# Layernorm of a linear-attention and FFN kernel: feature-major statistics on TensorE, or token-major bn_stats with a DMA transpose

## What is computed

```python
xn = _layernorm(x, axis=-1)                      # mean and variance over 1024 features
# recurrence, per batch: q, k, v = xn@Wq, xn@Wk, xn@Wv (64 wide); g = sigmoid(xn@Wg + bg)
#   S = decay * S + outer(k*g, v*g); out_t = q_t @ S;  s = outs @ Wo + bo
# feed-forward, int8-valued weights stored as int32, scale 1/127, hidden 3072:
#   h = silu(xn@wg.T) * (xn@wu.T);  g = silu(h@wd.T)
return x + s * g
```

## Time and profile before

| | us |
|---|---|
| median of 2 runs (716.69 and 722.12) | 719.41 |
| the profiled execution's own time | 720.41 |
| its span on the slowest core (core 2) | 718.8 |
| spans of the 8 cores | 708.5 to 718.8 |
| TensorE matmul busy | 602.2 |
| VectorE busy | 265.7 |
| ScalarE busy | 169.4 |
| GpSimd busy (issuing DMAs for the most part) | 73.4 |

### The profile page before, as it was taken

How to read it: one execution, slowest core, us unless ns; L and a number is a source line. 1 busy time by engine, 2 the same in 40 slices (tenths; PEclk the granted TensorE clock), 3 DMA queues, 4 the chain that set the end, 5 groups by cost and what they waited for, 6 DMA issues and landing times.

```text
span 718.8 us, 8478 instructions; the slowest of 8 cores (708.5 to 718.8 us)
## 1 busy us (share of the span) xinstructions
PE 602.2 (84%) x2939; PEld 288.4 (40%) x2996; DVE 265.7 (37%) x477; ACT 169.4 (24%) x268; POOL 73.4 (10%) x146
## 2 busy tenths in 40 slices
PE   0451877969884997988889999899999999999997
PEld 0320433535452444543434343344444444444443
DVE  2457076748886225453221222221112211122222
ACT  0541165545662021300100000111111111101100
POOL 5010212101110100110100000011111111000000
PEclk9975979889997899999999999999999999999999
DMA  8970788675651421323323132354544545012232
GB/s 165 177 119 1 111 117 133 101 125 67 109 89 31 77 40 31 50 45 54 45 44 118 59 118 72 104 81 67 87 68 79 83 66 88 1 58 101 76 117 89
DMA packets 24747, 58.63 MB, mean 82 GB/s; under 512 B 2753, under 2 KB 2881, under 8 KB 24706
## 3 DMA queue, kind: packets, MB, share of 16 engines
q0 software_dynamic: 19584, 39.85, 36.4%
q1 hardware_dynamic: 4608, 16.78, 6.6%
q10 hardware_dynamic: 514, 1.45, 0.8%
HBM read 89.53 MB, written 8.39 MB: 136 GB/s over the span
## 4 chain that ended last, share of the span: by engine, by line
PE 69%; DMA 11%; DVE 9%; issue 6%; ACT 3%; POOL 1%; DVEq 0%; ACTq 0%; POOLq 0%
PE pb L712 39%; PE pb L780 23%; DMA xstage<-xfm 7%; DMA xstage<-xpfm 4%; DVE abig L394 3%; PE pb L506 2%; DVE xn L398 1%; DVE wd_bf L398 1%; PE pb L796 1%; ACT xsqf L307 1%; PE pb L539 1%; ACT abig L814 1%; PE pb L423 1%; POOL wd_bf L279 1%; POOL gubf L679 1%
## 5 line engine op out<-in xcount | busy, mean ns | idle before, releaser
L712 PE MATMUL pb<-xn,gubf 128*128 128x512 bf16 x1495 | 351.0, 392 | 37.2 <-DVE xn L398 23.1
L712 PEld LDWEIGHTS pb<-xn,gubf 128*128 128x128 bf16 x1536 | 152.4, 101 | 223.0 <-issue 61.0
L780 PE MATMUL pb<-wd_bf,h_bf 128*128 128x512 bf16 x752 | 169.0, 379 | 9.5 <-ACT abig L814 5.9
L739 DVE SCALAR_TENSOR_TENSOR h_bf<-pb,sgbf 128x512 bf16<-128x512 f32 x96 | 66.1, 691 | 247.6 <-PE pb L712 213.7
L734 ACT ACTIVATE sgbf<-pb 128x512 bf16<-128x512 f32 x96 | 56.9, 593 | 275.6 <-PE pb L712 275.6
L780 PEld LDWEIGHTS pb<-wd_bf,h_bf 128*128 128x128 bf16 x768 | 74.4, 98 | 101.4 <-issue 12.8
L679 POOL DMA_DIRECT2D gubf<-wgu x96 | 50.9, 537 | 484.3 <-PE pb L712 369.2
L823 DVE TENSOR_TENSOR abig<-abig,pb 128x512 f32<-128x512 f32 x32 | 22.0, 688 | 137.9 <-ACT abig L814 82.0
L814 ACT ACTIVATE abig<-pb 128x512 f32<-128x512 f32 x32 | 19.1, 598 | 167.0 <-PE pb L780 167.0
L307 ACT ACTIVATE xsqf<-xstage 128x1024 bf16<-128x1024 bf16 x32 | 31.9, 1048 | 67.0 <-DMA xstage<-xpfm 34.2
L158 ACT ACT_TABLE_LOAD x32 | 41.1, 1283 | 0.6
(11 more groups left out here) (85 smaller groups left out, 206.3 us busy)
## 6 DMA issues: line engine op xcount, KB each, us to landing
gubf<-wgu POOLq DMA_DIRECT2D x96, 256.0 KB, 4.9
xtmt<-xtm SPq DMA_DIRECT2D x16, 512.0 KB, 4.0
out<-xtmt SPq DMA_DIRECT2D x16, 512.0 KB, 2.9
wd_bf<-wdt POOLq DMA_DIRECT2D x24, 256.0 KB, 8.8
xstage<-xfm POOLq DMA_DIRECT2D x8, 512.0 KB, 11.8
xstage<-xpfm POOLq DMA_DIRECT2D x8, 512.0 KB, 9.2
abig<-wqk ACTq DMA_DIRECT2D x1, 512.0 KB
xtmt<-wkvg ACTq DMA_DIRECT2D x1, 512.0 KB
```

The costliest lines, as they stand in the source:

```text
L712: e.matmul(out=o, lhsT=gu_bf[gpar][:, gu * 1024 + dc * 128: gu * 1024 + (dc + 1) * 128], rhs=xn[:, dc * N + half * 1024 + nh * 512: dc * N ...
L739: e.scalar_tensor_tensor(out=h_bf[:, hc * 1024 + nh * 512: hc * 1024 + nh * 512 + 512], in0=a, scalar=QS, in1=sg_bf[:, sgp * 512:(sgp + 1) ...
L780: e.matmul(out=o[:, dh * 512:(dh + 1) * 512], lhsT=h_bf[:, hc * 1024 + nc2 * 128: hc * 1024 + (nc2 + 1) * 128], rhs=wd_bf[:, hc * 1024 + d ...
```

## The change

The layernorm is turned to the token-major layout, in 32 tiles of 128 tokens.

- The host sends x once, token-major, as `xttm`: 32 tiles of 128 tokens by 1024 features, f32, own tokens first. The residual at the end reads the same tensor.
- `lnA_p(q)` loads a tile on SyncE's queue, with no cast, three tiles in flight.
- `lnB_p(q)`: two bn_stats of 128x512 on VectorE. `lnC_p(q)`: bn_aggr, a Sqrt of 128x1 on ScalarE, a reciprocal of 128x1, and one tensor_scalar of 128x1024 (f32 to bf16) that subtracts the mean and multiplies. There are two buffers `xhb` for its result, so tile q waits for the transpose of tile q-2.
- `lnD_p(q)`: SyncE issues a DMA transpose (SBUF to SBUF, 128x1024 bf16) into `xn`, or for a previous tile into `wd_bf`, waits for its completion, and raises the semaphore `YT` with a nop. What waited for VectorE's last operation on a tile waits for `YT` now (`f_e1`, `kvg_chunk`, `sum_chunks`, `qk_pass`).
- Gone are the squares, the 256 statistics matmuls, the variance on 128x256, the long reciprocal and the four TENSOR_TENSOR operations for each 256 tokens.
- The order of the tiles is 8 own, 16 previous, 8 own (`TOR`). The decay chain and the casts of the small weights become entries of `pre` (`decay_pre` at k = 3, `stage_pre` at k = 4), behind the first tiles.
- `pre` has two entries for a tile of 128 tokens. Slice 0 of the feed-forward stands behind the transpose of tile 3, slice 1 behind that of tile 7, and slices 2 to 24 carry the rest of layernorm.

The core of the diff (`decay_pre` holds the old decay chain, with a vector of ones of its own in place of `vtmp`; `kvg_chunk` holds the old matmuls and copies of `lnB_c`):

```diff
-    xfm = nc.dram_tensor("xfm", [8, 128, NDC * TL], F32, kind="ExternalInput").ap()
-    xpfm = nc.dram_tensor("xpfm", [8, 128, NDC * TL], F32, kind="ExternalInput").ap()
-    xtm = nc.dram_tensor("xtm", [N, D], F32, kind="ExternalInput").ap()
+    xttm = nc.dram_tensor("xttm", [32, 128, D], F32, kind="ExternalInput").ap()
...
-        xstage = [E_(nc.sbuf_tensor(f"xstage{i}", [128, NDC * TL], BF16)) for i in range(3)]
-        xsq_f = [E_(nc.sbuf_tensor(f"xsqf{i}", [128, NDC * TL], BF16)) for i in range(2)]
-        m_sb = [E_(nc.sbuf_tensor(f"msb{i}", [128, TL], F32)) for i in range(2)]
+        xts = [E_(nc.sbuf_tensor(f"xts{i}", [128, D], F32)) for i in range(3)]
+        xhb = [E_(nc.sbuf_tensor(f"xhb{i}", [128, D], BF16)) for i in range(2)]
+        stc = [E_(nc.sbuf_tensor(f"stc{i}", [128, 16], F32)) for i in range(2)]
+        ones_r = E_(nc.sbuf_tensor("ones_r", [1, 128], F32))
...
+        for dst, src in [(dec_s[:], dec), (bgs_s[:], bgs)]:
+            s.op(lambda e, d_=dst, s_=src: e.dma_start(out=d_, in_=s_), dDC, 16)
+        dec_done = dDC.n
...
+        def decay_pre():
+            s.wait(dDC, dec_done)
...
+            t.wait(S, s_ld)
+            t.wait(V, v_const)
+            t.op(lambda e: e.matmul(out=pb[3][:, 0:1], lhsT=ones_r[:],
+                                    rhs=ld_s[:], start=True, stop=True))
...
+        def stage_pre():
+            v.wait(dSM, smalls_done)
+            v.op(lambda e: e.memset(outsa[M:M + 1, :], 1.0))
+            v.op(lambda e: e.memset(S_bf[0][:], 0.0))
+            v.op(lambda e: e.tensor_copy(out=wqk_bf[:], in_=abig[:]))
+            v.op(lambda e: e.tensor_copy(out=wkvg_bf[:, 0:1024],
+                                         in_=xtmt[0][:]))
+            v_w1 = v.op(lambda e: e.tensor_copy(out=wkvg_bf[:, 1024:1280],
+                                                in_=xtmt[1][:, 0:256]), V, 1)
+            s.wait(V, v_w1)
+            s.op(lambda e: e.dma_start(out=abig[0:M + 1, :], in_=wob),
+                 dSM, 16)
+            smalls2 = dSM.n
+            v.wait(dSM, smalls2)
+            v.op(lambda e: e.tensor_copy(out=wob_bf[:], in_=abig[0:M + 1, :]),
+                 V, 1)
+            stg8["v_wsmall"] = V.n
...
+        TOR = list(range(8)) + list(range(16, 32)) + list(range(8, 16))
+
+        def lnA_p(q):
+            p3 = q % 3
+            if q >= 3:
+                y.wait(V, ap32[q - 3])
+            y.op(lambda e, d_=xts[p3][:], s_=xttm[TOR[q]]:
                  e.dma_start(out=d_, in_=s_), dX[p3], 16)
+            x_issue[q] = dX[p3].n
+
+        def lnB_p(q):
+            p3 = q % 3
+            par = q % 2
+            v.wait(dX[p3], x_issue[q])
+            if q >= 2:
+                v.wait(S, s_sig[q - 2])
+            v.op(lambda e, o=stc[par][:, 0:6], a=xts[p3][:, 0:512]:
+                 e.bn_stats(out=o, in_=a))
+            v_red[q] = v.op(lambda e, o=stc[par][:, 6:12],
+                            a=xts[p3][:, 512:1024]:
+                            e.bn_stats(out=o, in_=a), V, 1)
+
+        def lnC_p(q):
+            p3 = q % 3
+            par = q % 2
+            c = stc[par]
+            v.wait(V, v_red[q])
+            v_agg = v.op(lambda e, o=c[:, 12:14], a=c[:, 0:12]:
+                         e.bn_aggr(out=o, in_=a), V, 1)
+            s_pre("Sqrt")
+            s.wait(V, v_agg)
+            s_sig[q] = s.op(lambda e, o=c[:, 14:15], a=c[:, 13:14]:
+                            e.activation(out=o, in_=a, func=AF.Sqrt,
+                                         bias=eps_c[:]), S, 1)
+            v.wait(S, s_sig[q])
+            v_rc = v.op(lambda e, o=c[:, 14:15]:
+                        e.reciprocal(out=o, in_=o), V, 1)
+            v.wait(V, v_rc)
+            if q >= 2:
+                v.wait(YT, q - 2 + 1)
+            ap32[q] = v.op(
+                lambda e, o=xhb[q % 2][:], a=xts[p3][:], m=c[:, 12:13],
+                r=c[:, 14:15]:
+                e.tensor_scalar(out=o, in0=a, scalar1=m, scalar2=r,
+                                op0=OP.subtract, op1=OP.mult), V, 1)
+
+        def lnD_p(q):
+            t2 = TOR[q]
+            own = t2 < 16
+            y.wait(V, ap32[q])
+            if own:
+                dst = bass.AP(xn, t2 * 128,
+                              [[NDC * N, 128], [N, NDC], [1, 128]])
+            else:
+                pt2 = t2 - 16
+                par = (pt2 // 2) % 2
+                j = pt2 % 2
+                if pt2 >= 4:
+                    y.wait(T, kvgp_mm[2 * ((pt2 - 4) // 2) + j])
+                dst = bass.AP(wd_bf, (20 + 2 * par) * 1024 + j * 128,
+                              [[NHC * 1024, 128], [TL, NDC], [1, 128]])
+            y.op(lambda e, d_=dst, a=xhb[q % 2][:]:
+                 e.dma_start_transpose(out=d_, in_=a), dTR, 16)
+            y.wait(dTR, dTR.n)
+            y.op(lambda e: e.nop(), YT, 1)
+
+        def kvg_chunk(cc):
+            tt = cc // 2
+            j = cc % 2
+            par = tt % 2
+            kvg_ps = (pb[2] if j == 0 else pb[3])[
+                :, par * 512 + 256: par * 512 + 256 + 129]
+            t.wait(YT, 8 + cc + 1)
+            t.wait(V, stg8["v_wsmall"])
+            if cc < 2:
                 t.wait(V, st8["v_preexp"])
+            if cc >= 2:
+                t.wait(V, kvgp_evac[cc - 2])
+            t_mm = None
...
-            t.wait(V, apply_done[7])
+            t.wait(YT, 32)
             if idx >= 2:
                 t.wait(V, qk_evac[idx - 2])
             else:
-                t.wait(V, apply_done[15])
...
-        for k in range(19):
-            if k - 3 >= 0 and k - 3 < 16:
-                pre.append(lambda ti=k - 3: lnB_c(ti))
-            if k - 2 >= 0 and k - 2 < 16:
-                pre.append(lambda ti=k - 2: lnB_p(ti))
-            if k - 1 >= 0 and k - 1 < 16:
-                pre.append(lambda ti=k - 1: (lnA_c(ti), emit_wd_loads(2)))
-            if k < 16:
-                pre.append(lambda ti=k: lnA_p(ti))
+        pretag = []
+
+        def ln_bcde(k):
+            if 0 <= k - 1 < 32:
+                lnB_p(k - 1)
+                emit_wd_loads(1)
+            if 0 <= k - 2 < 32:
+                lnC_p(k - 2)
+            if 0 <= k - 3 < 32:
+                lnD_p(k - 3)
+            if 0 <= k - 11 < 16:
+                kvg_chunk(k - 11)
+
+        for k in range(36):
+            if k < 32:
+                pre.append(lambda q=k: lnA_p(q))
+                pretag.append(("A", k))
+            if k == 3:
+                pre.append(decay_pre)
+                pretag.append(("DY", 0))
+            if k == 4:
+                pre.append(stage_pre)
+                pretag.append(("SG", 0))
+            pre.append(lambda k=k: ln_bcde(k))
+            pretag.append(("D", k - 3))
...
-            t.wait(V, apply_done[half * 4 + nh * 2 + 1])
+            t.wait(YT, (4, 8, 28, 32)[half * 2 + nh])
...
         pre[0]()
+        pre[2]()
         load_gu(0)
         pre[1]()
-        pre[2]()
-        load_gu(1)
         pre[3]()
         pre[4]()
+        load_gu(1)
         pre[5]()
+        pre[6]()
         load_gu(2)
-        for fn in pre[6:10]:
+        cut1 = pretag.index(("D", 3)) + 1
+        cut2 = pretag.index(("D", 7)) + 1
+        for fn in pre[7:cut1]:
             fn()
         ffn[0]()
-        for fn in pre[10:16]:
+        for fn in pre[cut1:cut2]:
             fn()
         ffn[1]()
-        pi = 16
+        pi = cut2
```

More of the change, by code:

```diff
@@ L752, in f_e2 @@
             else:
[L753 to L755 removed]
+                y.wait(V, stg8["v_wsmall"])
+            y.op(lambda e, dpar=nc2 % 2, i2=idx2:
+                 e.dma_start(out=xtmt[dpar][:], in_=xttm[i2]),
                  dXT[nc2 % 2], 16)
@@ L774, in f_e2 @@
                     t.wait(S, s_fs[idx2 - 2])
+            if idx2 == 0:
+                s.wait(V, stg8["v_wsmall"])
+                t.wait(V, stg8["v_wsmall"])
             def dn_group(dh):
```

334 lines of the change are left out of this document (95 added, 239 removed).

## The result

The changed kernel takes 806.01 us (median of 11 runs, 795.87 to 815.69), the one before 719.33 (10 runs, 716.69 to 722.12), side by side on the same chips. The ratio is 1.114, with a 95% interval of 1.110 to 1.118: slower. The prediction, 695 with a range of 658 to 775, was wrong in sign and in range.

A forecast was written before the change was run, and what follows sets the result against it. It put the 242 us of layernorm at stake, mostly TensorE's chain with waits for VectorE. Layernorm's end at 213.5, then 124 for the old stretch and 357.9 of unchanged feed-forward gave 695 us, range 658 to 775.

The forecast's parts named there:

- I take L = 4.9: Price chosen for each DMA transposition: 4.9 us, as for 256 KB in ordinary traffic, with ends 3 and 8.3.
- L: Time from the end of a tile's tensor_scalar to the raised `YT`, including issue of the next x load and the transposition.
- L + 8.2: Layernorm round of two slices: transposition, key/value product, feed-forward slice, VectorE's statistics and tensor_scalar; 6.55 us a slice, 16 slices.
- The clock: Term of 4 us added to layernorm for TensorE's granted clock of 0.87, at which a slice costs 4.0 us.
- Wrong: List of signs against the forecast: transposition 7 us or more, TensorE's clock low throughout layernorm, bn_stats above 0.7 us.
- The start: Before the first feed-forward slices: first slice forecast at about 41 us, second at 62.5, where 46.15 and 68.5 were.
- The rest: After layernorm: old stretch with one more feed-forward slice, 124 us, then unchanged feed-forward work, 357.9 us.
- floor of 4.7 us: Least time a layernorm slice takes when no transposition is waited for: Silu, product, bn_stats, bn_aggr, Sqrt and table load.
- 128 x 305 ns: Statistics matmuls removed from TensorE: 128 at 305 ns and as many just like them, given as 40 us.
- SyncE's queue becomes the bound: Rival, 0.28: load, transposition and wait, one tile at a time, set layernorm's end; slower, 771 us at 8.3, possibly over 800.
- L + 0.4: SyncE's round for one tile, 0.4 for issuing: 5.3 us, for 7 slices without a key/value product.
- The rival at 0.18: Rival, 0.18: the transposition in layernorm hides no better than what it replaces, 5.4 to 7 us each; 705 to 734 us.

The follow-up runs named there:

- e10: Changed kernel with the load of x issued behind the transposition's completion instead of directly ahead of it: 767.40 us.
- e5: Changed kernel with down-weight loads moved behind layernorm and gate/up loads of chunks 3 to 14 cut to 16 of 128 partitions: 746.12 us.
- e1: Changed kernel with the 20 down-weight loads that stood in layernorm moved behind it: 787.55 us.
- e9: Changed kernel with TensorE transposing by identity matmuls, key/value product one slice later, down-weight loads behind layernorm, five buffers for x: 687.19 us.
- e11: e5 with the key/value product two slices later as in e3: 706.76 us.
- e2: Changed kernel with the DMA transposition replaced by a plain DMA copy in runs of 256 bytes, no transposing: 791.82 us.
- e12: Changed kernel with the gate/up loads issued one slice later, all transfers else the same: 773.10 us.
- e8: Changed kernel with the DMA transposition replaced by a plain copy in runs of 2 KB, no transposing: 760.55 us.
- e3: Changed kernel with the key/value product of a previous tile two slices later in TensorE's stream: 761.29 us.
- e13: Changed kernel with the edits of e1, e3 and e10 together: 747.96 us.
- e7: Changed kernel with the edits of e1 and e3 together: 745.48 us in one execution.

## Why the prediction was wrong, point by point

- **The step that failed is "I take L = 4.9".** The row it leaned on, 256 KB in 4.9 us, is the right size for a quiet queue: a transposition lands in 4.2 to 4.4 us from 52 to 78, in 3.05 alone (e10), in 5.4 with thin weights (e5). But the chain asks for L at the moment when GpSimd's loads have just been released too, and there the landing alone takes 9.6 to 16.0 us on the slowest core and 8.6 to 11.8 in e1; L as a whole is 13.0 in the round at 119 us. I had the high end at 8.3, from SyncE's one load under load. That a median over ordinary traffic might not do for a transfer which the kernel starts together with others could have been asked of the order of the program.
- **The sign does not hang on the slow core.** The other seven cores end at 760.5 to 770.2 us in the profiled execution, still above the 708.5 to 718.8 of before. On core 0 the transpositions of previous tiles on the chain take 5.5 to 11.8 us. On these cores the range would have held, the forecast of a gain would not.
- **The round.** L + 8.2 for two slices has the right members. From 95.5 to 242.2 us there are six rounds of two slices, 24.5 us each where 13.1 were forecast: 68 of the 110 us. In the round at 119 us the excess of 10.6 is 8.1 of transposition (L is 13.0, from the end of the tensor_scalar at 118.45 to the product at 131.46), 2.4 of slice and 0.4 of product, less 0.3 on VectorE.
- **The clock** was a term of 4 us, at 0.87. It was 0.72 from 82.3 to 260.8 us, as "Wrong" had named it for regular pauses: behind the waits of 11 to 17 us the product took 1.02 us instead of 0.62 and the first slice 4.7 to 6.1 instead of 3.62, together 2.4 us a round, some 14 us over the six. The row that the prediction read as a burst after a long pause, 6.08 us at 92.24, stands behind a pause of 0.33 us and did not show that. In e5, L is 6.6 us on average over eight rounds; the prediction's sum gives 729 for it, and 746 was measured. A round took 16.7 us there where L + 8.2 is 14.8: over eight rounds 15 of the 17 us, most of it product and slice at the lower level.
- **The start.** Forecast 41 and 62.5 us, measured 57.14 and 82.30. The first two transpositions on the chain, 22.57 and 12.43 us, fell into the weight burst; I had charged 4.9 each. Without the down loads (e1) the first slice started at 42.45 and the second at 67.02, so the rest of that account was nearly right. Slice 1 and the stretch from 242.2 to layernorm's end, with own tiles of which the chain's first took 11.48 us, give the remaining 19 us.
- **The rest.** 124 + 357.9 = 482 us were forecast for what follows layernorm, 805.6 - 320.3 = 485.3 were measured. In sum: 20 for the start, 87 up to layernorm's end, 3 behind it, 110 or so above 695.
- **The terms that held:** bn_stats 0.69 us (0.7), bn_aggr 0.19 (0.2), reciprocal 0.16 (0.2), the DMA-free floor of 4.7 us (5.16 in e9, which adds half a tile out of PSUM on ScalarE, 0.6 us). The tensor_scalar took 0.813 us (0.7), Sqrt 0.296 (0.2): together 0.2 us a tile. VectorE's busy time fell by 39.7 where I had 25, TensorE's by 25.2 where I had 40. The 40 was the busy time of the rows; "128 x 305 ns" twice would be 78, and does not belong in a sum of overlapping matmuls.
- **The rivals.** "SyncE's queue becomes the bound", at 0.28, named the right transfer and the right sign, and its "over 800 if a transpose costs more than any row" met the time, by luck: its mechanism is not what binds. SyncE's queue itself waited 56.8 us for a tensor_scalar, and TensorE 101.6 us at the key/value product: the bound is the forecast's own chain of two slices, with one long transposition in each round and one short. By the prediction's own terms the queue binds where L + 0.4 passes (L + 8.2)/2, from L = 7.4 and not 7, if every transposition is as long. The rival at 0.18 gave the reasons that counted, a fresh load ahead and GpSimd's 256 KB at 6.0 us, but I kept 4.9 in the sum. e11, where transpositions land in 4.7 us at the median and the look-ahead is longer, is the one DMA version below the kernel before.

What is shown: a landing is as long for a copy as for a transposition (e2); traffic of the weights (e1 12 us, e12 26, e5 44 beyond e1), the order of load and transposition on the queue (e10, 32), small pieces (e8, 33) and the short look-ahead (e3, 39) each carry a part. They overlap in part: e13 joins e1, e3 and e10 and is no faster than e7 without e10. What is not shown: how the DMA engines share their turns. The Trainium skill, "DMA: Bandwidth & Descriptors", section "Queues, rings and completion order", says that each engine goes round the queue rows that have work, a packet at a time. If so, a transfer in many small packets would wait behind as many of the others' large ones; e8's 33 us fit that inference, and no run here looked at single packets.

## What to carry to other kernels

A transfer on a short chain has to be priced by what the program issues in the same microsecond, not by the median of its queue; look for an event from which both paths start. When such a chain pauses TensorE, add the burst at the lower clock to each round, and look first at whether the consumer can ask one or two slices later. And for 128x1024 bf16 tiles in this kernel, which streams weights, eight small matmuls with an identity were a better transposition than the DMA.

## What the runs showed of the hardware that was not expected

- The DMA share is no measure of this delay: it was 0.66 both where every second transposition took 9.6 to 16.0 us (the changed kernel, 82 to 261 us) and where slices ran every 5.16 us (e9), and 0.62 before.
- The same SBUF-to-SBUF transfer of 256 KB took 3.05 us alone, 4.2 with a 512 KB load issued 0.45 us ahead, 9.6 to 16.0 when 1 MB of weights was issued with it, 4.1 to 5.8 half a round later on the same core, and 22.57 in the start's burst.
- Cores that run one program on as much data came apart by 43 us, and which cores they were, one or up to four, changed from one execution to the next. On the slow one of the profiled execution the weights' issue fell on the transposition's round after round; e12, which only moves that issue, took the spread to 17.5 us, e9 to 1.9.
